# A loop of TensorE with two groups of matmuls in exchanged order and its first instruction 18 program slots later

## The reference

```python
def attn_layer(x, Wqkv, qs, ksc, Wo):          # DEPTH 6, HEADS 16, DIM_HEAD 64, WINDOW 32
    q, k, v = split(x @ Wqkv)                  # heads apart
    q = l2norm(q) * qs
    k = l2norm(k) * ksc
    q = q * cos * scale + rotate_half(q) * sin * scale
    k = k * cos / scale + rotate_half(k) * sin / scale
    out = local_attention(q, k, v)             # softmax over the own and the previous window
    return out @ Wo
def ffn_layer(x, g, bln, W1, b1, W2, b2):
    a, gate = split(layernorm(x) * g + bln) @ W1 + b1
    return a * gelu(gate) @ W2 + b2
```

## Time and profile before

| what | us |
|---|---|
| median of 3 runs | 4722.76 |
| lowest and highest of them | 4708.98, 4727.22 |
| the profiled execution | 4691.7 |
| its span | 4689.9 |
| stretch of the 45 turns of the loop on TensorE, 450 to 4135 | 3685.0 |

### The profile page before, as it was taken

One profiled execution on the slowest core, in us unless ns is written; L12 is line 12 of the kernel. 1 busy time (PEld: TensorE's weight loads), 2 busy tenths in 40 slices (PEclk: granted clock), 3 DMA queues, 4 the chain that ended last, 5 costly groups with the idle time before them and its releaser, 6 DMA issues. The chain is left out here.

```text
span 4689.9 us, 172910 instructions
## 1 busy us (share of the span) xinstructions
PE 3973.2 (85%) x68188; PEld 2844.2 (61%) x68188; DVE 3168.6 (68%) x6779; ACT 3110.2 (66%) x8351; POOL 867.3 (18%) x1240
## 2 busy tenths in 40 slices
PE   7968888888888888888888888888888888885678
PEld 4746666666666666666666666666666666663334
DVE  4856776666667666666767666666766676665665
ACT  4836776777777677777767777776777777672233
POOL 0012122122121212112122112121211212110122
PEclk9979999999999999999999999999999999996689
DMA  0034344444334444334444434434444443430000
GB/s 28 1 80 83 75 83 83 87 88 85 77 77 80 96 88 83 79 74 83 92 88 80 82 78 86 92 78 81 83 83 91 82 81 77 80 74 17 3 5 12
DMA packets 126144, 336.58 MB, mean 72 GB/s; under 512 B 32592, under 2 KB 33744, under 8 KB 125264
## 3 DMA queue, kind: packets, MB, share of 16 engines
q0 software_dynamic: 61440, 201.38, 23.6%
q1 hardware_dynamic: 64080, 125.25, 10.6%
HBM read 22.41 MB, written 2.10 MB: 5 GB/s over the span
## 5 line engine op out<-in xcount | busy, mean ns | idle before, releaser
L1173 ACT ACTIVATE loc_probs<-loc_pair,loc_ebias,loc_rnorm 128x64 f32<-128x64 f32 x3072 | 1201.2, 434 | 9.7 <-DVE loc_ebias L1333 7.3
L919 PE MATMUL loc_pair<-loc_hs,loc_wqk 128*128 128x256 f32 x3072 | 748.9, 387 | 27.7 <-issue 19.5
L1173 ACT ACTIVATION_READ_ACCUMULATOR loc_probs<-loc_pair,loc_ebias,loc_rnorm 128x1 f32 x3072 | 723.9, 236 | 0.0
L919 PEld LDWEIGHTS loc_pair<-loc_hs,loc_wqk 128*128 128x128 f32 x3072 | 567.3, 192 | 128.4 <-issue 42.6
L1331 DVE TENSOR_REDUCE loc_mx<-loc_pair 128x8 f32<-128x512 f32 x384 | 264.8, 689 | 469.5 <-PE loc_pair L965 466.6
L868 POOL DMA_DIRECT2D loc_ks<-loc_msin x384 | 331.5, 1008 | 1230.2 <-DVE loc_msin L1281 1193.8
L1155 ACT ACTIVATE loc_sq<-loc_pair 128x1024 f32<-128x1024 f32 x384 | 397.2, 1034 | 211.5 <-PE loc_pair L919 211.5
L868 POOL DMA_DIRECT2D loc_qr<-loc_msin x384 | 332.1, 1006 | 1079.1 <-DVE loc_msin L1281 1061.4
L1281 DVE SCALAR_TENSOR_TENSOR loc_msin<-loc_pair,loc_scal,loc_tab 128x1024 f32<-128x1024 f32 x384 | 490.1, 1276 | 2.1 <-DMA loc_ks<-loc_msin 2.1
L965 PE MATMUL loc_pair<-loc_kr,loc_qr 64*32 64x64 f32 x24576 | 311.0, 226 | 121.8 <-issue 121.8
L965 PEld LDWEIGHTS loc_pair<-loc_kr,loc_qr 64*32 64x32 f32 x24576 | 263.3, 106 | 220.2 <-issue 219.9
(11 more groups left out here) (232 smaller groups left out, 7271.8 us busy)
## 6 DMA issues: line engine op xcount, KB each, us to landing
loc_ks<-loc_msin POOLq DMA_DIRECT2D x384, 256.0 KB, 4.5
loc_qr<-loc_msin POOLq DMA_DIRECT2D x384, 256.0 KB, 5.1
loc_veven<-loc_vodd SPq DMA_DIRECT2D x768, 64.0 KB, 3.5
loc_veven<-loc_vodd SPq DMA_DIRECT2D x384, 128.0 KB, 3.9
loc_wqk<-wqk_dram SPq DMA_DIRECT2D x12, 512.0 KB, 4.2
loc_wv<-wv_dram SPq DMA_DIRECT2D x6, 512.0 KB, 5.9
loc_wo<-wo_dram SPq DMA_DIRECT2D x6, 512.0 KB, 3.5
x<-xT_dram SPq DMA_DIRECT2D x1, 2048.0 KB, 7.4
```

The costliest lines, as they stand in the source:

```text
L919: ins = nc.tensor.matmul(pairs[b][:, p // 2, (p % 2) * UNIT:(p % 2 + 1) * UNIT], wqk[:, k, w:w + P], hs[u.odd][:, :], start=True, stop=True)
L1173: ins = nc.scalar.activation(probs[x][:, p, hp, :], pairs[b][:, hp, p * 2 * WIN:(p + 1) * 2 * WIN], ACT.Exp, bias=ebias[x][:, k:k + 1], sc ...
```

## The change

TensorE's step calls `weighted(0)` ahead of `spread(0)` in place of behind it, each with its own waits. And TensorE's loop starts at slot 226 of a block in place of 208.

```diff
             with nc.Fori(FILL // 2, TOTAL // 2, engines=bass.OrderedEngineSet([eng.engine]), hint_back_edge=True,
-                         head_slot={eng.engine: 208} if eng is nc.tensor else None) as i:
+                         head_slot={eng.engine: 226} if eng is nc.tensor else None) as i:
...
+                if at(3) is not None:
+                    vacated(pe, ((rot, at(1), 8, 2), (rot, at(2), 8, 8), (oT_ready, at(4), 2, 2),))
+                    weighted(0, at(3), 1)
                 if at(2) is not None:
                     vacated(pe, ((exp_ready, at(3), 4, 4), (rot, at(2), 8, 6),))
                     spread(0, at(2), 2)
-                if at(3) is not None:
-                    vacated(pe, ((rot, at(1), 8, 2), (rot, at(2), 8, 8), (oT_ready, at(4), 2, 2),))
-                    weighted(0, at(3), 1)
```

## The result

| | before | changed |
|---|---|---|
| median of 4 runs, us | 4719.11 | 4942.61 |
| lowest and highest | 4708.98, 4727.22 | 4937.9, 4954.52 |
| ratio, 95% interval | | 1.0479 (1.045 to 1.0507) |

A forecast was written before the change was run, and what follows sets the result against it. PE bounds the kernel, its work plus gaps, the largest being stops for 16 KB instruction blocks. Terms 3.5 + 1.6 + 0 + 0.3 = 5.4 us a turn, 243 us in 45 turns, on 4691.7: 4935, said as 4940, range 4780 to 5010.

The forecast's parts named there:

- (a): Loop's end and head: a thirteenth block adds one border before the head; +3.5 us a turn, bounds 3.1 and 3.9.
- (b): ffn_out now behind border 1|2, so values(0) comes 1.9 us later; +1.6 us a turn, bounds 0.9 and 2.0.
- (c): Exchange, first half: the stop in weighted(0) and later key scaling leave no gain; 0 us a turn, bounds -0.9 and +1.1.
- (d): Exchange, second half, no border stopping PE: key scaling starts later, PE waits for DVE; +0.3 us a turn, bounds 0 and 0.5.
- not before another 3.9: In (a): the head's block can be asked for only at border 11|12, so the head starts 3.9 us later.
- If the fetch of block 3 moves with PE's program: In (b), at border 2|3 in scores(1): then the whole 1.9 us stays; with the fetch unmoved, 1.3.
- It moves to 2530.9: In (c): the end of weighted(0)'s stop at border 4|5, 3.6 us behind a start 1.1 us earlier.
- If that fetch comes when it did, scores end as before.: In (c), at border 5|6 in scores(0): the later mask is hidden by the stop; 0 us.
- it still does: Upper bound of (c): the fetch of block 6 still sits behind the wait for the outputs; +1.1 us a turn.
- the hint: Rival at the loop's head: a hint hides the thirteenth block's cost; chance 0.13.
- The faster rival: Borders cost only where they stop PE now, and the exchange pays: L946's 81 us go, 4610 us; chance 0.04.
- The head did move: Against the rival that the loader sets the head elsewhere, (a) and (b) falling away: within 0.5% of 4700; chance 0.04.

The follow-up runs named there:

- x2: Kernel before with only the loop's head moved from slot 208 to 226, order as before: 4869.44 us, ratio 1.0338.
- x1: Kernel before with only the exchange of weighted(0) and spread(0), head still at slot 208: 4806.3 us, ratio 1.0216.
- x7: Kernel before with the exchange, and DVE's outputs(0) ahead of scale_keys(0), head at 208: 4738.98 us, ratio 1.0076.
- x6: Kernel before with the exchange and the head at slot 218, still 12 blocks: 4804.63 us, ratio 1.0211.
- y4: Kernel before with the exchange, head at 208, but spread(0)'s wait for ACT's exponentials put ahead of weighted(0): 4863.66 us, ratio 1.0334.

## Why the prediction was right, and where two terms were wrong

The total was right, 5.4 us a turn predicted against 5.5 in the profiled execution. That it is so near is luck: the head's terms (a) and (b) were 230 us and measured 155, the exchange's (c) and (d) were 14 us and measured 92 with the head at 208, 73 with it at 226. The errors cancel.

- **(a), +3.5: mechanism right, mis-sized.** Measured +4.4 in the changed kernel, +4.8 in x2, above the bound of 3.9. Of the two turnarounds in it the first was right: from border 10|11 to 11|12 the mean is 82.31 - 78.96 = 3.35 us, predicted 3.58. The second, "not before another 3.9", was wrong: from border 11|12 to the head it is 87.46 - 82.31 = 5.15 us. Before, from border 10|11 to the head, it was 81.91 - 77.89 = 4.0. The queue's records show where: the head's block is fetched 1.0 us behind the last border before, and 1.9 us behind it now. A last block that holds little but the branch doesn't get the head asked for sooner. The Trainium skill says (page "Runtime: NRT & Kernel Launch", section "Instruction fetch mechanics") that a taken branch to a block outside the loaded ones has to fetch it before execution goes on; these 5.15 us agree.
- **The clock at the head** was in no term. `project(2)` takes 3.57 us on average in place of 1.92, at half the clock. It costs nearly nothing more, since the next block comes no sooner: border 0|1 is passed at 3.60 against 3.48, and the stop of 1.5 us there is gone.
- **(b), +1.6: wrong size.** At `project(3)` +0.2 are left. `values(0)` comes 1.2 us later (8.38 against 7.22), near what was said, but the step "If the fetch of block 3 moves with PE's program" failed the other way: the fetch comes earlier, at 10.5 us of the turn in place of 12.6, and the stop in `scores(1)` is gone. In the runs with the head at 208, 218, 226 and 150 that fetch starts at 12.6, 13.7, 10.5 and 14.1. Border 1|2 lies ahead of the 16 slots of `probs_across(0)` by 40, 50, 58 slots in the first three, and this group waits for ACT. The group starts at 10.6, 11.8 and 11.8: at 208 and 218 the fetch comes 2.0 us behind its start, at 226 ahead of it. So the point of the program at which this block is asked for seems to lie ahead of the wait at 226, and in or behind it at the other two, which puts it some 50 to 57 slots into the block before. This is an estimate from three heads at one border; no run confirms it at another. The prediction named this as the weak place and didn't count the slots.
- **(c), 0: wrong.** +1.3 us by the table, +1.6 in x1, above the bound of +1.1. Its first step, "It moves to 2530.9", was nearly right in the changed kernel: the stop in `weighted(0)` ends 0.8 us earlier in the turn (34.86 before, 34.05 after), where 1.1 were forecast. The failed step is the one behind it, "If that fetch comes when it did, scores end as before." The fetch of block 6 comes 1.4 us later (39.7 in place of 38.3). `spread(0)`, which before lay in front of the stop, lies behind it, and all that hangs on it comes late: DVE's outputs end at 38.4 in place of 36.6, the mask starts at 39.2 in place of 37.3, and the stop in `scores(0)` ends at 42.1 in place of 40.8. The prediction had this chain and its last bound ("it still does") and chose the other end. On top of it comes the clock: in the 13 turns at full clock there the outputs end at 37.7, near the 37.6 of the prediction's 2534.9, in the others at 38.6.
- **In x1 the first step of (c) fails too.** The early start by 0.9 us moves the stop's end by 0.4 only (34.86 to 34.45), since the fetch of block 5 starts at 31.9 in place of 32.0; in the changed kernel it starts at 31.6. Counted from the start of `weighted(0)` that fetch comes after 1.3 us in x1 and x7, where the group begins at slot 10 of its block, after 0.9 in x6 (slot 20) and after 1.0 in the changed kernel (slot 28). The slots themselves don't explain it, since 18 of them are 0.1 us of this group. In the order of before, where the transpositions run right in front of the group, it comes after 0.5, 0.1 and 0.25 us (head at 208, 218, 226).
- **(d), +0.3:** the stretch to the second `outputs_across(0)` grew by 0.1 in x1. The wait for ACT turned into waits for DVE, as said.
- **Not in the sum:** the borders' other places give back 0.4 us in the second half and 0.5 in the first (x2 against before).

The rivals: the hint doesn't hide the block (4.5 us ahead of L919 in 44 turns). The faster rival had both its conditions against it, in x1 and x2. The head did move.

Open: when a block is asked for, and so why x1's early `weighted(0)` doesn't bring the fetch of block 5 forward while a later one delays it (y4, 32.5). The profile doesn't show how far TensorE's program is ahead of its matmuls. And no run sets the clock, so its share in the cost of the exchange and of head 150 is read from sorted turns.

## What to carry to other kernels

Count the blocks that a hot loop's program covers before moving its head or adding to its body: here two instructions across a border cost 5%, nine short of it nothing that can be told. Where an engine stops for its next block, the place of that stop decides what reordering is worth: the same exchange cost 92, 91 and 0 us at three heads. Here it paid to have work that releases another engine in front of the stop. And measure the parts of a change alone: a total right to 0.1% hid an error of 75 us in the head and one of 60 to 80 us, the other way, in the exchange.

## What the runs showed of the hardware that was not expected

- PE's granted clock fell to half behind a stop of 4 to 5 us at the head (0.50 over 3.75 us, from 2458.95), and also behind a stop of 2.05 us (changed kernel) or 2.51 us (x1) inside a turn. In x1 1.4 us of work stood between that stop and the 0.65 us of idle time before it. In the kernel before, a stop of 2.23 us at the same place came behind 2.5 us of work, and there 5 turns of 44 show the half clock, against 35 of 44 in x1.
- From one border to the next it took 3.35 us (10|11 to 11|12, mean in the changed kernel) and 3.58 us (0|1 to 1|2) with a stop at the second, and 5.15 us to a head that is reached by a branch from a nearly empty block. The transfer itself is 1.1 us of that. In the kernel before, the fetch of each of the loop's blocks starts when PE has passed into the block ahead of it, on average 0.1 to 5.5 us behind that border, so it is at most one block ahead.
- Nine semaphore increments more in each of 45 turns cost 5 us together (x3, ratio 1.001 with an interval from 0.9993 to 1.0027), which can't be told from nothing.
